# A two-layer graph network on one core: masked attention weights as the larger of two exponentials instead of a leaky ReLU and one exponential

## The reference

```python
h = relu(layernorm(x))                                   # layer 0
x = x + relu(concat(h, max over the first 25 neighbours of h) @ W0 + b0)
h = relu(layernorm(x)) @ W1                              # layer 1
s1, s2 = h @ a1, h @ a2
e = leaky_relu(s1[:, :, None] + s2[:, None, :], 0.4)
att = softmax(where(adj > 0, e, -1e20), axis=1)          # over the first node index
x = x + gelu(einsum('bij,bjo->bio', att, h))
```

## Time and profile before

| | |
|---|---|
| median of 3 runs | 4289.71 us (4282.42 to 4291.24) |
| the profiled execution | 4286.7 us, its span 4284.9 us |
| POOL | 3099.6 us busy (72%) |
| DVE | 3347.2 us busy (78%) |
| PE | 2678.6 us busy (63%) |
| ACT | 1963.2 us busy (46%) |

### The profile page before, as it was taken

One profiled execution on the slowest core, in us unless ns is written; L12 is line 12 of the kernel. 1 busy time (PEld: TensorE's weight loads), 2 busy tenths in 40 slices (PEclk: granted clock), 3 DMA queues, 4 the chain that ended last, 5 costly groups with the idle time before them and its releaser, 6 DMA issues. The chain is left out here.

```text
span 4284.9 us, 43700 instructions
## 1 busy us (share of the span) xinstructions
PE 2678.6 (63%) x13568; PEld 1997.2 (47%) x13568; DVE 3347.2 (78%) x7261; ACT 1963.2 (46%) x2364; POOL 3099.6 (72%) x3205
## 2 busy tenths in 40 slices
PE   2334446666666676566666666666666666666669
PEld 2222235444454554455444544455445445545457
DVE  5666689966898669986799768996689866998655
ACT  4222255632665236643466325553256532664146
POOL 5777777777777777777777777777777777777720
PEclk8555556777777777777777777777777767777779
DMA  6555556666666766666666666667666666666531
GB/s 211 169 158 181 175 183 215 209 221 217 204 214 208 232 214 196 216 219 227 202 217 204 224 214 214 216 198 230 209 213 219 206 220 225 193 214 203 175 109 55
DMA packets 412751, 860.10 MB, mean 201 GB/s; under 512 B 67299, under 2 KB 248422, under 8 KB 396134
## 3 DMA queue, kind: packets, MB, share of 16 engines
q0 software_dynamic: 153600, 419.64, 31.8%
q1 hardware_dynamic: 258918, 437.67, 30.2%
HBM read 714.43 MB, written 142.61 MB: 200 GB/s over the span
## 5 line engine op out<-in xcount | busy, mean ns | idle before, releaser
L411 POOL DMA_INDIRECT gb<-h_table,idx x3200 | 3098.9, 968 | 1012.2 <-issue 962.1
L980 PE MATMUL ps_av<-hz,lk 128*128 128x256 f32 x3712 | 1123.1, 469 | 118.6 <-DVE hz L817 118.6
L730 DVE TENSOR_REDUCE hl<-gb 128x256 f32<-128x3328 f32 x128 | 740.5, 5785 | 401.5 <-DMA gb<-h_table,idx 401.1
L980 PEld LDWEIGHTS ps_av<-hz,lk 128*128 128x128 f32 x3712 | 884.7, 245 | 351.9 <-issue 192.1
L730 DVE TENSOR_REDUCE gb<-gb 128x256 f32<-128x3328 f32 x128 | 748.6, 5848 | 10.5 <-DMA gb<-h_table,idx 10.5
L1035 PE MATMUL ps_l<-cf,hl 128*128 128x128 f32 x512 | 117.5, 373 | 673.9 <-issue 485.2
L1039 PE MATMUL ps_l<-w,hcat 128*128 128x256 f32 x1024 | 455.0, 622 | 86.4 <-ACT hcat L542 86.4
L542 ACT COPY hcat<-ps_l 128x512 f32<-128x512 f32 x128 | 74.9, 585 | 832.3 <-PE ps_l L1035 832.3
L428 ACT ACTIVATE sg<-ps_c 128x1024 bf16<-128x1024 bf16 x256 | 259.9, 1015 | 377.1 <-PE ps_c L956 358.3
L1035 PEld LDWEIGHTS ps_l<-cf,hl 128*128 128x128 f32 x512 | 77.1, 187 | 720.6 <-issue 720.6
L1039 PEld LDWEIGHTS ps_l<-w,hcat 128*128 128x128 f32 x1024 | 307.5, 314 | 194.3 <-ACT hcat L542 130.5
(11 more groups left out here) (130 smaller groups left out, 3634.9 us busy)
## 6 DMA issues: line engine op xcount, KB each, us to landing
ad<-in_adj SPq DMA_DIRECT2D x128, 1024.0 KB
p_rest<-lk SPq DMA_DIRECT2D x112, 512.0 KB, 3.5
lk<-p_rest SPq DMA_DIRECT2D x112, 512.0 KB, 4.1
gb<-h_table,idx POOLq DMA_INDIRECT x3200
edges_t<-stage SPq DMA_DIRECT2D x32, 1024.0 KB, 7.0
edge<-edges_t SPq DMA_DIRECT2D x64, 512.0 KB, 6.7
xl<-in_x SPq DMA_DIRECT2D x128, 128.0 KB, 5.5
hl<-h_table SPq DMA_DIRECT2D x128, 128.0 KB, 5.7
```

The source lines that it names most:

```text
L411: pool.indirect_dma_start(gb[c][:, s + (c > 0), :], None, table[tb], bass.IndirectOffsetOnAxis(idx[u][:, k:k + 1], 0)).then_inc(gathered[c ...
L730: V.tensor_reduce(dst, gb[c][:, :, :].rearrange("p k c -> p c k"), AX.X, ALU.max).then_inc(maxed[c], 1)
L980: ins = T.matmul(accumulator(k), lk_of(jj, u, drain)[:, k * P:(k + 1) * P], hz[jj][:, :], start=False, stop=False)
```

## The change

The exponential rises with its argument, so the exponential of a leaky ReLU is the larger of two exponentials, of v and of 0.4 v with v = value + s2. The change computes those two on ACT and takes the larger on DVE:

- `relu_part` and `exp_part` go; `exps` takes the first exponential of 2048 columns into `lk`, and the second in four pieces of 512 into the two banks of `ps_n`, which s1 has left. A piece waits until DVE has read the bank's piece before (`piece_read`, or `p_ready` for the last one of an item).
- The first two pieces follow the first exponential at once. The last two (`second_exp(..., 1)`) stand further back in ACT's list: behind the copy of `hcat` for the item with `jj` 1, and at the step's end for the item with `jj` 0.
- `item_leaky` becomes `item_max`: four pieces of `lk` against a bank, with the sum of each piece; `item_rows` adds the four sums.
- `item_bounds` is done for one item at a time, right behind its values, with one operation more (the second bias).
- s1 lies whole in SBUF in all rounds, and s2 is taken at the start of step 0.
- In the drain the second exponential is one of 2048 columns in place in `val`, and DVE reads both from SBUF.
- The mask's constant goes from 1e30 to 2 to the power 100.

```diff
-            def relu_part(i, j, jj, u, drain):
-                act.wait_ge(S["val_ready"], firsts(i) + 1)
+            def exps(i, j, jj, u, drain):
+                act.wait_ge(S["bounds_ready"], firsts(i) + 1)
                 act.wait_ge(S["av_done"], i - 2 if drain else i)
                 act.wait_ge(p_stored[jj], min(firsts(i) // 2, (NB - 1) * PAIRS) * 16)
...
+                nc.scalar.activation(lk_of(jj, u, drain)[:, :], val[jj][:, :], ACT.Exp, bias=nb[:, 1, bass.ds(j, 1)]
+                                     ).then_inc(S["exps_ready"], 1)
+                if i >= (NB - 1) * 32:
+                    nc.scalar.activation(val[jj][:, :], val[jj][:, :], ACT.Exp, scale=SLOPE, bias=nb[:, 0, bass.ds(j, 1)]
+                                         ).then_inc(S["piece_ready"], 1)
+                else:
+                    second_exp(i, j, jj, 0)
+
+            def second_exp(i, j, jj, half):
+                for p in range(half * HALF, half * HALF + HALF, PIECE):
+                    k = firsts(i) * (N // PIECE) + p // PIECE
+                    if k >= 2 and k % 4 == 1:
+                        act.wait_ge(S["p_ready"], k // 4)
+                    elif k >= 2:
+                        act.wait_ge(S["piece_read"], (k - 2) // 4 * 3 + (k - 2) % 4 + 1)
+                    nc.scalar.activation(ps_n[:, k % 2 * PIECE:(k % 2 + 1) * PIECE], val[jj][:, p:p + PIECE], ACT.Exp,
+                                         scale=SLOPE, bias=nb[:, 0, bass.ds(j, 1)]).then_inc(S["piece_ready"], 1)
...
                 if start:
                     blocked(it, (b - 1) * 4 + i, 0, u, drain and t > 0)
-                if rest and not drain:
-                    exp_part(it - 2, j2, 0, 1 - u, drain)
                 if rest:
-                    relu_part(it - 1, j1, 1, 1 - u, drain and t > 0)
+                    exps(it - 1, j1, 1, 1 - u, drain and t > 0)
...
+                if rest and it - 1 < (NB - 1) * 32:
+                    second_exp(it - 1, j1, 1, 1)
                 if fl is not None:
                     flush(fl)
...
+                if start and not drain:
+                    second_exp(it, j, 0, 1)
...
-                                                 in1=s1_of(i)[p // HALF][:, p % HALF:p % HALF + PIECE], scale=1.0, scalar=-3e38,
+                                                 in1=s1_all[:, p:p + PIECE], scale=1.0, scalar=-3e38,
...
+                n = o.mark(V.scalar_tensor_tensor(out=nb[:, 0, bass.ds(j, 1)], in0=m_a[:, 0, 0:1], scalar=0.0,
+                                                  in1=m_a[:, 1, 0:1], op0=ALU.min, op1=ALU.add))
+                dve.wait_ge(order, n)
+                V.tensor_tensor(nb[:, 1, bass.ds(j, 1)], nb[:, 0, bass.ds(j, 1)], s2p[:, bass.ds(j, 1)], ALU.add
+                                ).then_inc(S["bounds_ready"], 1)
...
                 for p in range(0, N, PIECE):
-                    ins = V.scalar_tensor_tensor(out=q[:, p:p + PIECE], in0=val[jj][:, p:p + PIECE], scalar=SLOPE,
-                                                 in1=q[:, p:p + PIECE], op0=ALU.mult, op1=ALU.add)
-                ins.then_inc(S["leaky_ready"], 1)
+                    k = firsts(i) * (N // PIECE) + p // PIECE
+                    dve.wait_ge(S["piece_ready"], k + 1)
+                    ins = V.scalar_tensor_tensor(out=q[:, p:p + PIECE], in0=q[:, p:p + PIECE], scalar=1.0,
+                                                 in1=ps_n[:, k % 2 * PIECE:(k % 2 + 1) * PIECE], op0=ALU.mult,
+                                                 op1=ALU.max, accum_out=z_p[:, jj, k % 4:k % 4 + 1])
+                    ins.then_inc(S["piece_read"] if p + PIECE < N else S["p_ready"], 1)
...
                 if sweep == 0:
-                    dve.wait_ge(S["exp_ready"], firsts(i) + 1)
+                    dve.wait_ge(S["p_ready"], firsts(i) + 1)
+                    n = o.mark(V.tensor_reduce(za[:, bass.ds(j, 1)], z_p[:, jj, :], AX.X, ALU.add))
+                    dve.wait_ge(order, n)
...
-                for h, part in enumerate(s1_of((b - 1) * 32)):
-                    o.mark(V.tensor_copy(part, s1_acc[:, h * HALF:(h + 1) * HALF]))
+                o.mark(V.tensor_copy(s1_all[:, :], s1_acc[:, :]))
```

More of the change, by code:

```diff
@@ L46 @@
 SLOPE = 0.4
-BLOCKED = 1e30
+BLOCKED = 2.0 ** 100
 PIECE = 512
@@ L153, in graph_layers @@
         m_a = sb("m_a", [P, 2, 2], fp32)
-        nb = sb("nb", [P, TILES], fp32)
+        nb = sb("nb", [P, 2, TILES], fp32)
+        z_p = sb("z_p", [P, 2, N // PIECE], fp32)
         za = sb("za", [P, TILES], fp32)
@@ L558, in step @@
                     evacuate_signs(v + 4, (v + 4) % 8 * P, 1)
-                if rest and not (drain and new):
-                    exp_part(it - 1, j1, 1, 1 - u, drain)
                 if l:
@@ L565, in step @@
                 if start:
[L566 to L570, removed]
+                    exps(it, j, 0, u, drain)
                 if t == 0 and new:
@@ new lines, in item_bounds, with item_max @@
+                dve.wait_ge(order, n)
+                V.tensor_tensor(nb[:, 1, bass.ds(j, 1)], nb[:, 0, bass.ds(j, 1)], s2p[:, bass.ds(j, 1)], ALU.add
+                                ).then_inc(S["bounds_ready"], 1)
+            def item_max(o, i, jj, u, drain):
+                q = lk_of(jj, u, drain)
+                dve.wait_ge(S["exps_ready"], firsts(i) + 1)
+                if i >= (NB - 1) * 32:
+                    n = (NB - 1) * TILES * (N // PIECE)
+                    dve.wait_ge(S["piece_ready"], n + firsts(i) - (NB - 1) * TILES + 1)
+                    for p in range(0, N, PIECE):
+                        k = p // PIECE
+                        ins = V.scalar_tensor_tensor(out=q[:, p:p + PIECE], in0=q[:, p:p + PIECE], scalar=1.0,
+                                                     in1=val[jj][:, p:p + PIECE], op0=ALU.mult, op1=ALU.max,
+                                                     accum_out=z_p[:, jj, k:k + 1])
+                    ins.then_inc(S["p_ready"], 1)
+                    return
+                for p in range(0, N, PIECE):
+                    k = firsts(i) * (N // PIECE) + p // PIECE
+                    dve.wait_ge(S["piece_ready"], k + 1)
+                    ins = V.scalar_tensor_tensor(out=q[:, p:p + PIECE], in0=q[:, p:p + PIECE], scalar=1.0,
+                                                 in1=ps_n[:, k % 2 * PIECE:(k % 2 + 1) * PIECE], op0=ALU.mult,
+                                                 op1=ALU.max, accum_out=z_p[:, jj, k % 4:k % 4 + 1])
+                    ins.then_inc(S["piece_read"] if p + PIECE < N else S["p_ready"], 1)
@@ L860, in step @@
                         take_s1(o, b)
+                        take_s2(o, b)
+                        dve.wait_ge(S["s_copied"], b)
                     if not sweep:
                         item_value(o, it, j, 0, drain)
+                        item_bounds(o, it, j, 0)
                 if old and drain and not before:
-                    item_leaky(o, it - 1, 1, 1 - u, drain)
+                    item_max(o, it - 1, 1, 1 - u, drain)
                 if old:
@@ L871, in step @@
                 if old and not drain and not before:
-                    item_leaky(o, it - 1, 1, 1 - u, drain)
-                if new and not t:
-                    take_s2(o, b)
+                    item_max(o, it - 1, 1, 1 - u, drain)
                 if words:
@@ L906, in step @@
                     item_value(o, it + 1, j + 1, 1, drain)
-                if new and sweep == 0:
-                    if not t:
-                        dve.wait_ge(S["s_copied"], b)
-                    item_bounds(o, it, j)
+                    item_bounds(o, it + 1, j + 1, 1)
                 if new and drain:
-                    item_leaky(o, it, 0, u, drain)
+                    item_max(o, it, 0, u, drain)
                 if old and t:
@@ L974, in av @@
                 if i % 32 < 16:
-                    pe.wait_ge(S["exp_ready"], firsts(i) + 1)
+                    pe.wait_ge(S["p_ready"], firsts(i) + 1)
                 else:
```

37 lines of the change are left out of this document (10 added, 27 removed).

## The result

The changed kernel took 4321.59 us (median of 4 runs, 4316.03 to 4323.7) beside 4290.33 for the one before: ratio 1.0074, interval 1.0059 to 1.0089. The profiled execution took 4320.31 us, its span 4318.5.

A forecast was written before the change was run, and what follows sets the result against it. POOL bounded the kernel before, and DVE would bound sweep 0 after. Profiled execution 4286.7 + 35 (seven rounds of 5) + 2 (drain) = 4323.7, stated as 4323 us; own range 4306 to 4340, overall range 4284 to 4350.

The forecast's parts named there:

- The bound: Sweep 0: DVE becomes the bound after the change, 33.3 us a step against POOL's 32.3; chance 0.55.
- The additions to a step: DVE in a step of sweep 0 (two items): 1.03 + 0.38 + 0.6 = 2.0 us more.
- the bounds: DVE, sweep 0: five operations for each item instead of four for both, 1.03 us a step more.
- the sums: DVE, sweep 0: adding the four sums, one dependent operation per item, 0.38 us a step more.
- the banks: DVE, sweep 0: the third piece waits for ACT to refill a bank, 0.3 us an item, 0.6 a step.
- the separate reads of the sums: DVE's larger-of-two: 0.07 us behind each piece, eight a step, taken as no difference, at most 0.6.
- A round: Sweep 0, to the first gather after its last reduction of chunk 0: 5 us later a round, 35 over seven.
- The drain: After the last gather: PE stays its bound at 6.91 us an item but starts later, +2 us.
- The GELU: First flush of the drain, on ACT: PE's start hangs on it, one more pass of 2.0 us ahead.
- Of the 1.3 us a tile that goes with them, a third falls away: Sweep 0 gathers, rival that POOL stays the bound with quicker gathers: 25 us less, 4264; chance 0.11.
- about 1 us: Sweep 0: what DVE can take on per step before it becomes the bound instead of POOL.
- rival 5: Drain: larger-of-two with two fp32 SBUF operands and a sum runs at halved throughput, DVE bounds, 26 us, 4350; chance 0.04.

The follow-up runs named there:

- no_sum: The changed kernel without the addition of an item's four sums, the reciprocal taking the first quarter's sum alone: ratio 1.0052 to the kernel before.
- no_banks_late: The changed kernel with the second exponential one operation in place, banks unused, the jj 1 item's placed behind the copy of hcat: 1.0035 to the kernel before.
- column_bound: The changed kernel with the exponent's bound from the largest s1 of all rows, once a round for all 16 items: ratio 0.9935 to the kernel before.
- column_bound_before: The kernel before with the bound from the largest s1 of all rows, once a round: ratio 1.0008.
- dose2: The kernel before with four small dependent DVE operations more in each of steps 1 to 8, none in the drain: ratio 0.9941, median 4262.12 us.
- dose5: The kernel before with ten small dependent DVE operations more in each of steps 1 to 8, none in the drain: ratio 1.0018.
- s1_whole: The kernel before with s1 whole in SBUF in all rounds, nothing else: ratio 1.0007.
- flush_first: The changed kernel with the drain's first flush (GELU) ahead of the second item's exponentials on ACT: ratio 1.0088 to the kernel before.
- both: column_bound with, in the drain, the first GELU ahead of the second item's exponentials and the first item's rows scaled before the second's larger-of-two: 0.9937 to the kernel before.
- leaky256: The kernel before with the leaky ReLU on DVE in eight pieces of 256 instead of four of 512: ratio 0.9982.
- no_banks: The changed kernel with the second exponential one operation of 2048 columns in place in val in all rounds, PSUM banks unused: ratio 1.0083 to the kernel before.

## Why the prediction was right, point by point

- **The bound.** DVE bounds sweep 0 after the change: its waits for gathers are gone, and taking work from it pays (no_sum, no_banks_late, column_bound), while in the kernel before it doesn't (column_bound_before). The phase is not what paid: the gathers lose 53 us in no_sum and in column_bound beside 57, and more, 72, in no_banks_late.
- **The additions to a step.** I summed 2.0 us; DVE's work grew by 1.8 (31.0 to 32.8). Of it the bounds measure 0.95 for 1.03, the sums 0.2 for 0.38, the banks 0.4 for 0.6. The rest, 0.2 to 0.3, I had at nothing, with a bound of 0.6 for the separate reads of the sums. They are there, but mostly hidden: the pieces follow at 0.61 instead of 0.60, 0.08 a step. What makes the remainder is not shown.
- **A round.** I had 5.0 us; the last gather ends 4144.2 us into the trace instead of 4112.4, 31.8 over seven rounds, 4.5 each. Step 1 began 1.0 later in the mean, for the 0.8 of the sum. The shortfall is in steps 2 to 6: they grew by 3.8 in the mean of the seven rounds (4.05 in round 4), for the 5.0 of the sum, to 33.1 us a step instead of 33.3.
- **The drain.** +2 in the sum; from the last gather to the end it takes 1.8 longer (172.5 to 174.3). This is not clear of the spread between traces: dose2, dose5 and s1_whole, whose drain is that of before, take 170.1 to 172.1. The GELU was named as the cause; flush_first and `both` show that its place is not what counts. ACT's list is full there, and that the second exponential is the pass too many in it is argued, not shown.
- **The banks.** DVE's third piece starts 0.23 late (predicted 0.3), behind ACT:

```profile
2225.72 0.68 DVE L821 SCALAR_TENSOR_TENSOR lk<-lk,ps_n 128x512 f32<-128x512 f32 x1
...
2226.56 0.69 DVE L821 SCALAR_TENSOR_TENSOR lk<-lk,ps_n 128x512 f32<-128x512 f32 x1 [0.15 <-ACT ps_n L514]
```

  0.84 us lie between these two (kernel after, step 3 of round 4), where pieces follow at 0.61.
- **What failed: the price of contention.** "Of the 1.3 us a tile that goes with them, a third falls away" took it for a rate per us of two SBUF operands, which gave 25 us; 22.6 came, but not for that reason. L806's holds went altogether (42.6 to 0), the values' rose from 19.9 to 36.5, and s1_whole shows that the additional SBUF operands alone don't raise them (18.1). That leaves their phase to the gathers. I also took POOL's 32.3 us a step for a fixed pace, and with it "about 1 us" of room on DVE. It was slow by holds; with them gone (dose2) a step takes 32.0, and POOL stops being the bound at smaller additions. That the forecast held is owed to additions large enough for DVE to bound at either pace, so that POOL's gain went into its waits: 85.3 us, not the 50 or so that I named.
- **Luck in the number.** The forecast of 4323 lies within 2 us of the median, closer than its terms. I added 37 us to the profiled execution of before, which lies 3.6 us below the median that the result has for it; the growth was 33.6 us between the two spans and 31.3 between the two medians.
- **The drain's larger-of-two** (rival 5): its four pieces with two fp32 operands in SBUF and a sum follow at 0.61 us, as the others do, so the halved rate quoted there does not show, and nothing turns over to DVE. Two of them in the kernel after:

```profile
4204.03 0.69 DVE L813 SCALAR_TENSOR_TENSOR lk<-lk,val 128x512 f32<-128x512 f32 x1
...
4204.65 0.69 DVE L813 SCALAR_TENSOR_TENSOR lk<-lk,val 128x512 f32<-128x512 f32 x1
```

## What to carry to other kernels

Where two engines run at nearly the same period, an edit on one moves the phase between them too, and that can be worth as much as the edit (dose2 gained 0.6% by it; the whole change cost 0.7%): add a small dose of idle work in the same place before crediting a gain to the edit. Work added to the engine that is second costs little while the other still sets the pace, and most of itself beyond: from dose2 to dose5, 1.1 us a step cost 35 us. Count the dependent small operations (0.15 to 0.19 us each) first: forming a bound once for 16 items instead of 16 times took 1.4% off the changed kernel, where DVE is the bound, and nothing off the kernel before. Where a pass is added to an engine, look for the stretch in which that engine is already the bound (ACT at the drain's start), not at its share of the span.

## What the runs showed of the hardware

A gather on POOL that starts inside a DVE operation with two operands in SBUF is held to about 0.12 us ahead of that operation's recorded end (leaky256: 224 gathers, spread 0.002 us; no_banks: 110 held, spread 0.003), and one that starts beside a piece with one operand in PSUM is not (L821: no block of four cost more than 0.02 us). The copy of s1 of 2048 columns (1.21 us), with one operand, holds too: 6 gathers of the kernel after by 0.76 us in the mean. A gather that runs already isn't stretched, and DVE isn't held by it: the gather at 1749.03 of dose2 takes 0.94 us and the block that starts 0.09 us behind it 2.49, as in the earlier trace rows.

The Trainium skill (SBUF — State Buffer, Who interferes with whom) calls the contention for the port pair that DVE shares with GpSimd an exclusive lock, and says of DVE's modes with two ports that "Whoever issues first gets the shared pair for the whole instruction; the other fully blocks (not throttle)". The runs agree as far as DVE issues first: the gather is held for what is left of the instruction, with two operands in SBUF too. They don't show that a gather blocks DVE; in dose2 it does not. The prediction gave the section's rule for a single SBUF input without its exception, the modes with two ports, among whose operations the section names copies; the copy of s1 agrees with the exception.
